# Graph attention, two layers, one core: who casts the first tables, and when the rows of x are turned, in block 0 of the first layer

## The reference, cut to what matters

```python
def _L0_gnn_ref(h, adj, a):            # N = 4096 rows, D = 64 columns
    src = h @ a[:D, 0]
    dst = h @ a[D:, 0]
    e = src[:, None] + dst[None, :]
    e = jnp.where(e > 0, e, 0.01 * e)
    e = jnp.where(adj > 0, e, NEG_INF)
    return jax.nn.softmax(e, axis=1) @ h

...
    x = _layernorm(x + _L0_gnn_ref(x, adj, L0_gnn_a), axis=-1)
    x = _layernorm(x + _L1_gnn_ref(x, adj, w, a, bias), axis=-1)   # the same over wh = x @ w, plus a bias
    return x
```

## Time and profile before

| | us |
|---|---|
| median of 3 runs | 512.29 (510.12 to 512.89) |
| the profiled execution, its own time | 511.4 |
| its span, first to last instruction | 509.3 |
| layer 1, loads of adj going on | to about 262 |
| TensorE busy over the span | 445.1 (87%) |
| VectorE | 403.8 (79%) |
| ScalarE | 397.6 (78%) |
| GpSimd | 97.0 (19%) |
| mean granted TensorE clock | 0.93 of full speed |

### The profile page before, as it was taken

The page is one execution under the profiler, slowest core; times in us unless marked ns, Lnnn a source line. Parts: engine busy times, 40 slices in busy tenths (PEclk is TensorE's granted clock), DMA queues, the critical chain, the costliest instruction groups (busy, mean ns, idle before and its releaser), DMA issues.

```text
span 509.3 us, 11866 instructions
## 1 busy us (share of the span) xinstructions
PE 445.1 (87%) x4420; PEld 414.6 (81%) x4420; DVE 403.8 (79%) x710; ACT 397.6 (78%) x619; POOL 97.0 (19%) x76
## 2 busy tenths in 40 slices
PE   0799677969989797998979989999999999989891
PEld 0488577959979796987979869999999998989791
DVE  3789989889898999999896989775665757574854
ACT  2794279777998889798864749889898989898941
POOL 0002221515134062523514200000101010101010
PEclk9997888997989899998979759999999999999897
DMA  7999999999999999999943001102021111202000
GB/s 194 255 239 281 282 268 292 320 287 333 296 334 315 327 331 307 335 313 318 315 139 126 1 1 42 42 14 82 17 78 30 63 46 47 69 23 88 6 12 10
DMA packets 80427, 87.59 MB, mean 172 GB/s; under 512 B 7440, under 2 KB 76304, under 8 KB 80400
## 3 DMA queue, kind: packets, MB, share of 16 engines
q1 hardware_dynamic: 45744, 53.01, 36.5%
q10 hardware_dynamic: 34656, 34.21, 24.5%
HBM read 77.78 MB, written 9.44 MB: 171 GB/s over the span
## 4 chain that ended last, share of the span: by engine, by line
issue 50%; DVE 22%; DMA 20%; PE 3%; POOL 3%; SPq 1%; ACT 1%; POOLq 0%; ACTq 0%; DVEq 0%
DMA stage<-in_adj 18%; DVE narrow L792 5%; DVE turned L804 3%; PE acc L420 2%; DVE pos L818 2%; POOL small L970 2%; DMA xn<-in_x 2%; DVE num L855 1%; DVE red L848 1%; DVE red L830 1%; DVE neg L821 1%; DVE num L862 1%; DVE kept L729 1%; DVE kept L804 1%; DVE num L852 1%
## 5 line engine op out<-in xcount | busy, mean ns | idle before, releaser
L558 ACT ACTIVATE neg<-srow,dcol 128x512 int8 (+1 forms) x512 | 353.0, 881 | 13.5 <-issue 10.0
L420 PE MATMUL acc<-xy_old,pos 128*128 128x195 bf16 x1024 | 196.3, 261 | 26.4 <-POOL pos L980 21.9
L420 PE MATMUL acc<-xy_old,neg 128*128 128x195 bf16 x1024 | 196.0, 261 | 0.0
L420 PE MATMUL acc<-stage,pos 128*128 128x195 bf16 x1024 | 179.5, 249 | 4.8 <-DVE red L830 4.8
L420 PE MATMUL acc<-stage,neg 128*128 128x195 bf16 x1024 | 179.4, 249 | 0.0
L420 PEld LDWEIGHTS acc<-xy_old,pos 128*128 128x128 fp8e4 x1024 | 106.5, 104 | 35.2 <-issue 33.6
L420 PEld LDWEIGHTS acc<-stage,pos 128*128 128x128 fp8e4 x1024 | 101.3, 99 | 9.9 <-issue 9.7
L420 PEld LDWEIGHTS acc<-xy_old,neg 128*128 128x128 fp8e4 x1024 | 105.9, 103 | 1.5
L420 PEld LDWEIGHTS acc<-stage,neg 128*128 128x128 fp8e4 x1024 | 100.7, 98 | 0.4 <-issue 0.3
L792 DVE TENSOR_SCALAR narrow<-stage 128x4096 uint8<-128x4096 int32 x32 | 74.5, 2329 | 12.5 <-DMA stage<-in_adj 11.7
L821 DVE TENSOR_TENSOR neg<-neg,kept 128x1024 uint32<-128x1024 uint32 x32 | 39.6, 1237 | 44.8 <-ACT neg L558 44.2
(11 more groups left out here) (115 smaller groups left out, 302.5 us busy)
## 6 DMA issues: line engine op xcount, KB each, us to landing
stage<-in_adj ACTq DMA_DIRECT2D x64, 512.0 KB, 8.9
stage<-in_adj SPq DMA_DIRECT2D x64, 512.0 KB, 9.3
spill<-turned SPq DMA_DIRECT2D x16, 512.0 KB, 7.1
turned<-spill SPq DMA_DIRECT2D x16, 512.0 KB, 3.6
out<-x1s SPq DMA_DIRECT2D x8, 128.0 KB, 1.9
xn<-in_x SPq DMA_DIRECT2D x1, 768.0 KB, 16.6
kept<-in_x SPq DMA_DIRECT2D x4, 128.0 KB, 3.7
kept<-in_x ACTq DMA_DIRECT2D x4, 128.0 KB, 4.8
```

Source lines behind the costliest of these rows:

```text
L420: last = nc.tensor.matmul(acc[:, r, c * XW:(c + 1) * XW], masks[c][:, t // BYTES, t % BYTES, r * P:(r + 1) * P], xy[layer][:, g * GT + t, ...
L558: last = nc.scalar.activation(o[:, t // BYTES, t % BYTES, :], srow[:, bass.ds((s % 2) * 512, 512)], ACT.Sign, bias=dcol[:, layer, col:col ...
```

## The change

- DVE no longer casts in block 0: `product0`, `rest_of_high0` and `low0` stay on DVE, `cast` on ACT makes the high and the middle part, with a semaphore each way (`part_ready`, `part_cast`). On DVE a granule's `to_bytes` and `turn` stand between the three.
- The tiles of x are loaded half by half (b outer), with a semaphore for each half; `dots0` and ACT's copy to `wh0` run per half.
- PE turns only blocks 0 and 1 before granule (0,0), with `spread_max0` between them. Blocks 2 and 3 follow granule (0,0), blocks 4 to 6 granule (0,1), block 7, the mean and half of the scores granule (0,2), through banks `flip` and `misc`. The other half of the scores follows granule (0,3).
- The six later blocks of the rows of x are loaded by two DMAs behind load (0,1) on SP's queue.
- ACT starts with three signs of granule (0,0) before `exps`; its copies of x, casts and signs are interleaved by hand, and `load_next` stands behind the signs and the casts of its granule.
- `row_factors0` and `source_vectors` on DVE, and `row_factors(0)`, `copy_weights`, `turn_weights` and PE's `source_vectors`, come later in block 1.

```diff
...
...
         def load_tiles(queue, quarters):
-            for a in quarters:
-                for b in range(GB):
+            for b in range(GB):
+                for a in quarters:
                     queue.dma_start(
                         h_raw[Q * a:Q * a + Q, :].rearrange("q (g b n) -> q g b n", g=NG, b=GB)[:, :, b, :],
-                        x.rearrange("(g a b q e) d -> a b q g (e d)", g=NG, a=NA, b=GB, q=Q)[a, b]).then_inc(s_h, 16)
+                        x.rearrange("(g a b q e) d -> a b q g (e d)", g=NG, a=NA, b=GB, q=Q)[a, b]).then_inc(s_h[b], 16)
...
             queue.dma_start(xn[:, :, :].rearrange("p (c h) d -> p c (h d)", h=2)[:, c],
-                            x.rearrange("(c p h) d -> p c (h d)", p=P, h=2)[:, c]).then_inc(s_x[c.start > 0], 16)
+                            x.rearrange("(c p h) d -> p c (h d)", p=P, h=2)[:, c]).then_inc(s_x[(c.start > 0) + (c.start > RB)], 16)
...
...
             load(sp, LOWER, 0, 0)
-            load_rows(sp, slice(RB, IB // 2))
             load(sp, LOWER, 0, 1)
+            load_rows(sp, slice(RB, 2 * RB))
+            load_rows(sp, slice(2 * RB, IB // 2))
             sp.dma_start(acol[:, 1:2], a1[0:D, :]).then_inc(s_w, 16)
...
...
             def turn_x(t):
-                if t >= RB:
-                    pe.wait_ge(xT_ready, t - RB + 1)
+                to = acc[:, t, :] if t < 2 else [flip, misc][t % 2][:, :]
+                if t > 3:
+                    pe.wait_ge(xT_ready, t - 1)
                 for b in range(RB):
-                    last = nc.tensor.transpose(acc[0:D, t % RB, b * P:(b + 1) * P],
+                    last = nc.tensor.transpose(to[0:D, b * P:(b + 1) * P],
                                                xn[:, t // 2 * (2 * RB) + t % 2 + 2 * b, :], idf[:, :])
...
...
                 w = SUP // D
-                pe.wait_ge(shift_ready, 1)
+                pe.wait_ge(xT_ready, NS - 1)
                 for b in range(0, IB, w):
...
...
             def scores0(half):
+                pe.wait_ge(xT_ready, NS)
                 for s in range(half * NS // 2, (half + 1) * NS // 2):
-                    pe.wait_ge(xT_ready, s + 1)
                     for r in range(RB):
...
...
                 pe.wait_ge(s_a, 32)
+                turn_max0()
                 pe.wait_ge(s_x[0], 16)
-                for t in range(2):
-                    turn_x(t)
-                turn_max0()
+                turn_x(0)
+                spread_max0()
+                turn_x(1)
                 pe.wait_ge(arep_ready, 1)
...
                 score_row(0, 0)
-                spread_max0()
                 pe.wait_ge(xT_ready, 2)
                 score_row(0, 1)
-                pe.wait_ge(s_x[1], 16)
-                for t in range(2, NS):
-                    turn_x(t)
-                mean0()
-                scores0(0)
-                pe.wait_ge(xT_ready, NS)
...
...
                 if first:
-                    turn_weights()
+                    scores0(1)
                 granule(0, s + 1, 0)
                 if first:
-                    source_vectors()
+                    turn_weights()
                 else:
...
                 granule(0, s + 1, 1)
+                if first:
+                    source_vectors()
                 if last:
...
...
             granule(0, 0, 0)
-            scores0(1)
+            pe.wait_ge(shift_ready, 1)
+            pe.wait_ge(s_x[1], 16)
+            for t in (2, 3):
+                turn_x(t)
             granule(0, 0, 1)
+            pe.wait_ge(s_x[2], 16)
+            for t in (4, 5, 6):
+                turn_x(t)
             granule(0, 0, 2)
+            turn_x(7)
+            mean0()
+            scores0(0)
             body0(0, first=True)
...
...
+            def raw(b):
+                return (wh0[:, :, 0:D].rearrange("p (g b e) d -> p g b e d", g=NG, b=GB)[:, :, b],
+                        h_raw.rearrange("p (g b e d) -> p g b e d", g=NG, b=GB, e=BYTES)[:, :, b])
             def tables0():
-                act.wait_ge(s_h, 16 * NA * GB + 16)
-                nc.scalar.copy(wh0[:, :, 0:D], h_raw.rearrange("p (t d) -> p t d", d=D)).then_inc(h_copied, 1)
+                for b in range(GB):
+                    act.wait_ge(s_h[b], 16 * NA)
+                    nc.scalar.copy(*raw(b)).then_inc(h_copied, 1)
                 for t in range(2):
                     copy_x(t)
+                signs(0, 0, 0, range(0, 3))
                 act.wait_ge(shift_ready, 1)
                 exps(0, slice(0, TILES), mcol[:, 2:3], mcol[:, 3:4], exp_ready)
-                signs(0, 0, 0)
                 load(act, UPPER, 0, 1)
-                for t in range(2, NS):
+                cast(0, 0)
+                signs(0, 0, 0, range(3, 6))
+                cast(0, 1)
+                signs(0, 0, 0, range(6, GT))
+                load_next(0, 0)
+                signs(0, 0, 1, range(0, 6))
+                cast(1, 0)
+                signs(0, 0, 1, range(6, GT))
+                cast(1, 1)
+                load_next(0, 1)
+                for t in (2, 3):
                     copy_x(t)
+                signs(0, 0, 2, range(0, 3))
+                cast(2, 0)
+                signs(0, 0, 2, range(3, 6))
+                cast(2, 1)
+                signs(0, 0, 2, range(6, GT))
+                load_next(0, 2)
+                for t in (4, 5, 6):
+                    copy_x(t)
+                signs(0, 0, 3, range(0, 3))
+                cast(3, 0)
+                signs(0, 0, 3, range(3, 6))
+                cast(3, 1)
+                signs(0, 0, 3, range(6, GT))
+                load_next(0, 3)
+                copy_x(7)
+            def cast(g, part):
+                t = slice(g * GT, (g + 1) * GT)
+                act.wait_ge(part_ready, 2 * g + part + 1)
+                nc.scalar.copy(xy[0][:, t, :, part, :].rearrange("p t c f -> p c t f"), rest0).then_inc(part_cast, 1)
...
                 act.wait_ge(xT_psum, t + 1)
-                nc.scalar.copy(xT_at(t), acc[0:D, t % RB, :]).then_inc(xT_ready, 1)
+                nc.scalar.copy(xT_at(t), acc[0:D, t, :] if t < 2 else [flip, misc][t % 2][0:D, :]).then_inc(xT_ready, 1)
...
...
                     if first and g == 1:
+                        row_factors(0)
+                    if first and g == 2:
                         copy_weights()
...
...
             tables0()
-            load_next(0, 0)
-            for g in range(1, NG):
-                signs(0, 0, g)
-                load_next(0, g)
-            row_factors(0)
             signs(0, 1, 0)
...
...
             def dots0():
-                dve.wait_ge(s_h, 16 * NA * GB + 16)
-                a = arow[:, D:2 * D].unsqueeze(1).broadcast_to((P, TILES, D))
-                temp = terms0[:, :, 0:D]
-                step(nc.vector.tensor_tensor(temp, h_raw.rearrange("p (t d) -> p t d", d=D), a, ALU.mult))
-                step(nc.vector.tensor_reduce(dcol[:, 0, :], temp, AX, ALU.add))
+                dve.wait_ge(s_row, 16)
+                a = arow[:, D:2 * D].unsqueeze(1).unsqueeze(1).broadcast_to((P, NG, BYTES, D))
+                for b in range(GB):
+                    dve.wait_ge(s_h[b], 16 * NA)
+                    temp = terms0[:, :, 0:D].rearrange("p (g b e) d -> p g b e d", g=NG, b=GB)[:, :, b]
+                    rows = h_raw.rearrange("p (g b e d) -> p g b e d", g=NG, b=GB, e=BYTES)[:, :, b]
+                    d = dcol[:, 0, :].rearrange("p (g b e) -> p g b e", g=NG, b=GB)[:, :, b]
+                    step(nc.vector.tensor_tensor(temp, rows, a, ALU.mult))
+                    step(nc.vector.tensor_reduce(d, temp, AX, ALU.add))
                 nc.vector.tensor_reduce(mcol[:, 0:1], dcol[:, 0, :], AX, ALU.max).then_inc(max_step, 1)
...
...
-            def tables0(g):
-                split(0, g, rest0).then_inc(tables_ready, 1)
+            def product0(g):
+                t = slice(g * GT, (g + 1) * GT)
+                shape = (P, 2, GT, E)
+                nc.vector.tensor_tensor(rest0, wh[0][:, t, :].unsqueeze(1).broadcast_to(shape),
+                                        wts[:, :, t].unsqueeze(3).broadcast_to(shape), ALU.mult).then_inc(part_ready, 1)
+            def part0(g, part):
+                return xy[0][:, g * GT:(g + 1) * GT, :, part, :].rearrange("p t c f -> p c t f")
+            def rest_of_high0(g):
+                dve.wait_ge(part_cast, 2 * g + 1)
+                nc.vector.tensor_tensor(rest0, rest0, part0(g, 0), ALU.subtract).then_inc(part_ready, 1)
+            def low0(g):
+                dve.wait_ge(part_cast, 2 * g + 2)
+                nc.vector.tensor_tensor(part0(g, 2), rest0, part0(g, 1), ALU.subtract).then_inc(tables_ready, 1)
...
...
                 for g in range(NG):
+                    if g == 2 and s == 0:
+                        row_factors0()
                     to_bytes(s + 1, g)
...
...
                         read_acc(0, s)
-                    if g == 2 and s == 0:
+                    if g == 3 and s == 0:
```

(23 more changed lines are left out.)

## The result

The changed kernel takes 519.7 us (median of 4 runs, 519.51 to 523.4) against 512.43 (4 runs, 510.12 to 512.89): a ratio of 1.017, 95% interval 1.013 to 1.020. It is 7 us slower; the forecast was 511.1 in a range to 515.5, so it was wrong, beyond the far end. The profiled execution took 519.51 us with a span of 517.4, 8.1 more than the span before.

A forecast was written before the change was run, and what follows sets the result against it. DVE was taken to set the pace in block 0, with DMA also near its limit. Narrow (1,0) 3.5 us early, 2.0 left at narrow (1,2), 1.2 after source_vectors: 511.1 us, range 507.5 to 515.5.

The forecast's parts named there:

- 16 scores (1.9): PE's chain ahead of row_factors0: each half of the scores, 16 matmuls, was to take 1.9 us.
- The score row: PE, between granule (0,3) and the second half of the scores: one score row was to take 0.6 us.
- the fed case: PE's granule after steady work takes 5.6 us at 247 ns a matmul, against 7.8 at 301 ns after thin work.
- The start of granule (0,2): PE's granule (0,2) in block 0 was to run from 51.3 to about 57.5 us, after DVE's masks end at 49.8.
- POOL has 1.2 us of product before the next narrow: Block 0: argument against rival B's POOL halves taking 3.15 us after the product, as they do beside a narrow.
- rival C: No gain because of DMA: ACT's load halves go out later and 9.1 us of waits swallow the gain; 512.3 us, chance 0.17.
- The head: Before granule (0,0): shift near 13.6 instead of 17.0, but exponentials end at 18.7 instead of 17.55, a loss of 1.2 us.
- The casts: ACT in block 0: each cast of 128x1040 was to take 1.05 us, between a floor of 0.70 and half of 1.90.
- 53.2 and 57.2: Start of narrow (1,0): 53.2 us with DVE alone, 57.2 with ACT's and PE's delays, 3.5 us early.
- The wait of 2.4 us for the first cast of granule (0,2): DVE in block 0, ready at 41.0 us, was to wait 2.4 us for ACT's cast, done at 43.4.
- `source_vectors`: DVE in block 1 was to wait 0.8 us here for PE's granule (1,1), leaving 1.2 us of gain.
- B: Slower: PE's scores ahead of row_factors0 end at 75.6 us, narrow (1,2) 1.8 late, 3.0 to 4 us lost, 515.5; chance 0.22.

The follow-up runs named there:

- e4: The changed kernel with 8 instead of 32 score matmuls, one per block of 512 rows written to four columns: 515.7 us, ratio 1.006.
- e9: The changed kernel with both a quarter of the score matmuls and ACT's halves of the loads issued as soon as the slot is free: 510.7 us, ratio 0.997.
- e3: The changed kernel with row_factors0 on DVE behind narrow (1,2) instead of ahead of it: 516.8 us, ratio 1.010 to the kernel before.
- e10: The changed kernel with its PE part undone, ACT's loads issued early, exponentials ahead of the signs and DVE's block 0 steps reordered: 507.1 us, ratio 0.988.
- e5: The changed kernel with ACT's halves of loads (0,3), (1,0) and (1,1) issued ahead of the second cast: 520.0 us, ratio 1.017.
- e12: The kernel before with all four quarters of every load issued by SP, none by ACT: 594.2 us, ratio 1.161.
- e2: The changed kernel without its casts on ACT, DVE splitting the tables itself again: 521.5 us, ratio 1.019 to the kernel before.

## Why the prediction was wrong, point by point

- **The step that failed: "16 scores (1.9)".** The earlier trace rows say x32 in 3.73 us, and I read 32 matmuls, so half of it for 16. The code issues 16 there, and the profile holds each twice: a half costs 3.73 at least, and measured 4.85 and 4.47. The score row (0.6 in the sum) was halved the same way: its two records take 1.12. Together 6.0 us in a chain with no slack.
- **The clock in granule (0,3).** I took 5.6 us, the fed case; it took 7.8 at 301 ns, behind scores of one column each, during which the granted clock fell. 2.2 us, and e4 and e9 show that it was these scores.
- **The start of granule (0,2)**, forecast for 51.3, was 53.31: DVE's masks ended at 50.93 instead of 49.8, and POOL's half behind them took 2.10 beside the product instead of 1.26. The granule took 7.1 instead of 6.2: PE had been idle for 3.24 us, and its granted clock was 0.50 from 54 to 56 us. The parts add up to 11.1 us, less 0.3 that the last turn didn't cost and what overlaps: the scores end at 82.14, not 71.8. e3, e4 and e9 show that this chain set the time.
- **POOL beside DVE.** "POOL has 1.2 us of product before the next narrow" missed that the product blocks POOL and POOL then blocks the narrow: 0.6 to 1.1 us on each of three narrows. In the changed kernel it also stands in PE's chain, by the 0.84 us on POOL's half of granule (0,2) and by what it adds to the time at which the masks end; no run takes it out there, and e9 is as fast as the kernel before with it in. In e10 its removal shows, together with better placed casts.
- **The load of (1,1).** That ACT's halves go out "1 to 2 us after SP's" stood in rival C, as a reason for no gain. Its price did not: with the earlier issue of this load and the two before it, narrow (1,1) starts 5.5 us sooner (e5). By which mechanism is open.
- **The head.** The dot products started at 7.42 and 9.94, not 6.3 and 8.83, and the maximum was there at 12.6. PE's turns of x now stand behind the turn of that maximum: they start at 12.95, and with them the first score row moves from 14.02 to 15.44, which I had left in its place. Shift at 14.90, forecast 13.6; exponentials done at 20.2, forecast 18.7. The product starts 2.7 us late, not 1.2, and narrow (0,1) starts at 31.95, not 29.9.
- **What held.** The casts: 1.05 to 1.08 us, forecast 1.05. Narrow (0,3) at 52.0 was forecast for 51; (0,2) at 41.3 came 2.3 late, and (1,0) at 60.09, forecast for 57.2, was just outside what I had set. In both 53.2 and 57.2 I had taken off 1.2 us for `row_factors0`, which the 8.8 us of a granule never held; the same 1.2 goes off because the product of granule (0,3) stands ahead of its narrow, so that sum was right by luck. The loss passed whole from 97 us on. The wait of 2.4 us for the first cast of granule (0,2) did not come, since that cast ended at 44.5 and the narrow of 3.36 at 44.7; 0.59 for the second remained. `source_vectors` waited for nothing.
- **The rivals.** B named the place and the point: it decides once PE ends its scores after 73.8. They ended at 82.1. With the scores priced right it would have been the forecast: 71.8 + 6.0 for scores and score row + 2.2 for the clock is 80.0, narrow (1,2) at 81.2 and a loss of 6.2 us where 8.35 was measured.

## What to carry to other kernels

Count the instructions of a term in the code, not only in the record, before dividing a row by them. A step moved behind other work on an in-order engine must be priced with everything it now stands behind, and with the clock that this work leaves. And where two gates stand at one point, an experiment on one of them shows little or nothing (e4 half, e5 nothing): only both together give the cause (e9). Before an effect is put down to one thing, such as the number of queues, look whether the experiment moved a second with it (e12).

## What the runs showed of the hardware that I had not expected

- With every load on one queue the engines moved 228 GB/s at a share of 1.11 (e12), with two 316 at 1.09; yet one queue alone moved 387 GB/s when it read rows of 4 KB into 128 partitions, and two moved 219 from 60 to 64 us in the changed kernel. The busy share says nothing of the rate, and in e12, from 97 to 262 us, SP's queue alone stands at 111.1%: it goes over 1 without two queues that overlap.
- POOL's subtraction and DVE's narrow, product or subtraction take turns whole: the one that started later adds what is left of the other (narrow 2.29 to 3.37, product 1.24 to 2.31, POOL 1.27 to 2.11 or 3.15). A transpose on DVE does not take part.
- A quarter of the score matmuls with four columns each took 1.05 us, against 3.73 at a granted clock of 1.00 (e2) and 4.85 where it fell: their time goes by their number, not by their columns.
